# First attention: value tiles of 32 columns held stationary, its output made transposed, probabilities normalised on GpSimd

## The reference

```
def lora_linear(x, W, b, Bm, Am):
    out = jnp.einsum('bld,od->blo', x, W) + b
    upd = jnp.einsum('blr,or->blo', jnp.einsum('bld,rd->blr', x, Bm), Am)
    return out + SCALING * upd
q = _split(lora_linear(x, Wq, bq, Bq, Aq))
k = _split(lora_linear(x, Wk, bk, Bk, Ak))
v = _split(lora_linear(x, Wv, bv, Bv, Av))
scores = jnp.einsum('bhqd,bhkd->bhqk', q, k) * SCALE
attn = jax.nn.softmax(scores, axis=-1)
out = jnp.einsum('bhqk,bhkd->bhqd', attn, v)
B, H, L, hd = out.shape
out = out.transpose(0, 2, 1, 3).reshape(B, L, H * hd)
return lora_linear(out, Wo, bo, Bo, Ao)
```

## Time and profile before

| | us |
|---|---|
| median of 3 runs | 1203.41 |
| lowest to highest | 1200.97 to 1204.36 |
| the profiled execution's own time | 1205.9 |
| its span, first to last instruction | 1203.7 |
| first attention, of that span | 0 to 249.7 |

### The profile page before, as it was taken

The page is one execution under the profiler, slowest core; times in us unless marked ns, Lnnn a source line. Parts: engine busy times, 40 slices in busy tenths (PEclk is TensorE's granted clock), DMA queues, the critical chain, the costliest instruction groups (busy, mean ns, idle before and its releaser), DMA issues. The chain is left out here.

```text
span 1203.7 us, 20980 instructions
## 1 busy us (share of the span) xinstructions
PE 1084.6 (90%) x7435; PEld 977.8 (81%) x7435; DVE 683.3 (57%) x1521; ACT 469.1 (39%) x1605; POOL 201.4 (17%) x151
## 2 busy tenths in 40 slices
PE   6898988879975369999999999999999799999977
PEld 4787877769875358988889988888988689999967
DVE  6667576836868754545454545544464465545554
ACT  2554555532304314444444444444444342322322
POOL 5101010323307421111111111111111110100010
PEclk9899999888988679999999999999999899999979
DMA  6000000000005210000000000000000050000002
GB/s 257 2 2 0 0 0 1 1 19 1 0 28 168 84 37 1 2 1 1 1 0 0 0 0 0 0 0 0 1 2 1 28 211 1 0 0 0 2 1 71
DMA packets 10502, 27.73 MB, mean 23 GB/s; under 512 B 1936, under 2 KB 6960, under 8 KB 9808
## 3 DMA queue, kind: packets, MB, share of 16 engines
q1 hardware_dynamic: 9152, 26.02, 6.2%
q10 hardware_dynamic: 1296, 1.00, 0.3%
HBM read 24.91 MB, written 2.10 MB: 22 GB/s over the span
## 5 line engine op out<-in xcount | busy, mean ns | idle before, releaser
L1105 POOL TENSOR_TENSOR wa_prob<-wa_prob,wa_rsum 128x512 f32<-128x512 f32 x64 | 66.9, 1045 | 444.0 <-DVE wa_rsum L1322 444.0
L41 PE MATMUL bank<-norm_xT_hi,wide_hi 128*128 128x512 f32 x256 | 106.7, 417 | 2.2 <-ACTq L1289 2.2
L1249 ACT ACTIVATE wa_prob<-wa_prob,wa_negmax 128x128 f32<-128x128 f32 x256 | 100.0, 391 | 17.2 <-DVE wa_negmax L1311 16.8
L1348 DVE TENSOR_TENSOR le_w_or_z_lo<-bank,le_w_or_z_hi 128x512 fp32r<-128x512 f32 x64 | 44.2, 691 | 106.8 <-ACT le_w_or_z_hi L1282 106.0
L453 ACT ACTIVATE la_prob<-bank,la_negmax 128x128 f32<-128x128 f32 x256 | 90.3, 373 | 37.1 <-DVE la_negmax L508 34.3
L43 PE MATMUL bank<-norm_xT_hi,wide_lo 128*128 128x512 f32 x256 | 101.8, 398 | 0.0
L42 PE MATMUL bank<-norm_xT_lo,wide_hi 128*128 128x512 f32 x256 | 101.6, 397 | 0.0
L1264 ACT COPY wa_v<-bank 128x512 f32<-128x512 f32 x64 | 37.4, 585 | 127.7 <-PE bank L43 127.7
L132 POOL TENSOR_TENSOR norm_rstd<-norm_rstd,minus_half 128x4 f32<-128x4 f32 x23 | 23.6, 1026 | 365.3 <-DVE norm_rstd L118 365.2
L1317 DVE COPY wa_k<-bank 128x512 f32<-128x512 f32 x64 | 44.2, 691 | 68.3 <-PE bank L43 68.3
L1257 ACT COPY wa_q<-bank 128x512 f32<-128x512 f32 x64 | 37.5, 586 | 115.6 <-PE bank L43 115.6
(11 more groups left out here) (276 smaller groups left out, 2842.3 us busy)
## 6 DMA issues: line engine op xcount, KB each, us to landing
le_raw<-in_wide_w SPq DMA_DIRECT2D x16, 512.0 KB, 4.5
em_w<-in_em_w SPq DMA_DIRECT2D x1, 4096.0 KB, 15.1
x<-in_x SPq DMA_DIRECT2D x4, 512.0 KB, 4.7
lc_kt<-in_ctx_rev SPq DMA_DIRECT2D x1, 2048.0 KB, 10.8
lc_toep<-in_toeplitz SPq DMA_DIRECT2D x1, 2048.0 KB, 14.2
out_x<-x SPq DMA_DIRECT2D x8, 256.0 KB, 2.9
li_kt<-in_ctx_rev SPq DMA_DIRECT2D x1, 1536.0 KB, 7.1
la_w_raw<-in_l_w SPq DMA_DIRECT2D x1, 1024.0 KB, 6.5
```

The source lines that it names most:

```text
L41: nc.tensor.matmul(out, a[0], b[0], start=start, stop=False, skip_group_check=True)
L1105: nc.gpsimd.tensor_tensor(prob[:, s], prob[:, s], rsum[:, s, :].unsqueeze(2).to_broadcast([P, G, P]), ALU.mult).then_inc(prob_ok, 1)
L1249: last = nc.scalar.activation(prob[:, s, j, :], prob[:, s, j, :], ACT.Exp, bias=negmax[:, s, j:j + 1], scale=SCALE, accum_out=sums[:, s, j ...
L1348: nc.vector.tensor_tensor(z[1][:, t % 2, :], b_z[:, :], z[0][:, t % 2, :].bitcast(F32), ALU.subtract).then_inc(z_lo, 1)
```

## The change

- `weigh` is turned round: a head's 32 columns (its own 16 and 16 of zeros) of v are stationary, the transposed probabilities move. The result of each of the four heads goes to its own 32 partitions of the bank, already transposed, so that `turn_o` and `o` are gone and ScalarE's `keep_o` casts straight from that bank. Heads that are neighbours in a quarter differ in parity and add up. Rows of the q and k weights are reordered on the host to fit.
- The probabilities are normalised before the turn: VectorE's `inverse_sums`, then GpSimd's `normalise` over 128x512. They have three buffers instead of two.
- The row maximum is one instruction (`negate=True`); the scale has moved into `parity`, and ScalarE evacuates q.
- q and k have two buffers by group. The next group's projections are in pieces: values in units 0 and 2, q in 4 and 6, k in 8 and 10, all through one bank; the transposes of the x after that in units 13 and 14. Group 1's x is prepared ahead of the loop.
- All is written out, no loop and no register waits; units run through the groups' borders. The output bias is added in quarters.
- v has its own place beside the convolution's products, and is cleared in one piece of 4096 columns. Group 2 has the products and squares in 16 pieces on GpSimd, one a unit; the skip terms stand one a unit in group 3.
- Ahead of the first unit q comes first, then k, then v.

```diff
+    def turn_chunk(self, pe, it, c, bank):
+        for j in range(G):
+            last = self.nc.tensor.transpose(bank[:, j * P:(j + 1) * P], self.xn[:, j, c * P:(c + 1) * P],
+                                            self.pr.ident[:])
+        last.then_inc(self.s_tr, 1)
+
+    def hi_chunk(self, act, it, c, bank, out=None):
+
+        act.wait_ge(self.s_tr, DC * (self.done(it) - 1) + c + 1)
+        self.nc.scalar.copy((self.xT[0] if out is None else out)[:, c, :], bank[:, :]).then_inc(self.s_hi, 1)
...
-        q = sb("q", [P, 2, DC, GT])
-        k = sb("k", [P, DC, GT])
-
-
-        DIAG = P + HD
-        v = pr.shared[:, 0:2 * (G * H * P + P)].rearrange("p (n c) -> p n c", n=2)
-        negmax = sb("negmax", [P, 2, 4])
-        sums = sb("sums", [P, 2, H])
-        rsum = sb("rsum", [P, 2, H])
-        prob = sb("prob", [P, 2, 4, P])
+        q = sb("q", [P, 2, 2, DC, GT])
+        k = sb("k", [P, 2, DC, GT])
...
+        VW = 2 * HD
+        at = 2 * GH * NPAIR
+        v = pr.shared[:, at:at + 2 * G * H * VW].rearrange("p (i j h c) -> p i j h c", i=2, j=G, h=H)
+        NP, NS = 3, 4
+        negmax = sb("negmax", [P, NS, 4])
+        sums = sb("sums", [P, NS, 4])
+        rsum = sb("rsum", [P, NS, 4])
+        prob = sb("prob", [P, NP, 4, P])
...
+        V_AT, Q_AT, K_AT, T_AT = (0, 2), (4, 6), (8, 10), (13, 14)
+        STATS_AT, APPLY_AT, BIAS_AT = 6, 8, 9
+        HI_AT, PROJECT_AT, ADD_AT = RG + 1, RG + 2, RG + 3
...
+            def add_bias(t, j):
+                pool.wait_ge(norm.s_xn, norm.done(t))
+                own = x[:, t * G + j, :]
+                nc.gpsimd.tensor_tensor(own, own, out_bias[:], ALU.add).then_inc(xb_ok, 1)
+
+            def normalise(n):
+                pool.wait_ge(r_ok, n + 1)
+                own = prob[:, n % NP]
+                nc.gpsimd.tensor_tensor(own, own, rsum[:, n % NS, :].unsqueeze(2).to_broadcast([P, 4, P]), ALU.mult)\
+                    .then_inc(prob_ok, 1)
+
+
+            PIECES = [(d, half) for d in range(CONV_C) for half in range(2)]
+            FIRST = N - U - len(PIECES)
+
+            def conv_piece(d, half):
+                own = conv_input(pr, 0)[:, half]
+                nc.gpsimd.tensor_tensor(pr.kk[:, half, :, OFF[d]:OFF[d] + CONV_C - d], own[:, :, 0:CONV_C - d],
...
+            for n in range(N - 1):
+                g, u = divmod(n, U)
+                normalise(n + 1)
+                if g + 2 < NG and u == STATS_AT:
+                    norm.pool_rstd(pool, g + 2)
+                if g + 1 < NG and BIAS_AT <= u < BIAS_AT + G:
+                    add_bias(g + 1, u - BIAS_AT)
+                if FIRST <= n < FIRST + len(PIECES):
+                    if n == FIRST:
+                        pool.wait_ge(pr.conv_loaded, 16 * 4)
+                    conv_piece(*PIECES[n - FIRST])
+                if g == NG - 1 and u == STATS_AT:
...
+            def scores(n):
+
+                t = n // U
+                if n % U == 0:
+                    pe.wait_ge(q_ok, DC * (t + 1))
+                    pe.wait_ge(k_ok, DC * (t + 1))
+                for d in range(2):
+                    wait(pe, exp_ok, n + d - RG + 1)
...
+                    last = nc.tensor.matmul(b_v[VW * s:VW * s + VW, r // 2 * P:r // 2 * P + P],
+                                            v[:, t % 2, j, head(r, s), :], probT[:, n % 2, s, :],
+                                            start=(r == 0), stop=(r == RG - 1), skip_group_check=True)
...
+                if u in V_AT:
+                    if u == V_AT[0]:
+                        pe.wait_ge(norm.s_lo, DC * norm.split(t))
+                    else:
+                        pe.wait_ge(v_ok, 2 * t + 1)
+                    values(t, V_AT.index(u), b_p[0])
+                if u in Q_AT:
+                    if u == Q_AT[0]:
+                        pe.wait_ge(v_ok, 2 * t + 2)
+                    else:
+                        pe.wait_ge(q_ok, DC * t + 1)
+                    q_or_k(t, Q_AT.index(u), 0, b_p[0], q_ps)
+                if u in K_AT:
+                    if u == K_AT[0]:
+                        pe.wait_ge(q_ok, DC * t + 2)
+                    else:
+                        pe.wait_ge(k_ok, DC * t + 1)
+                    q_or_k(t, K_AT.index(u), 1, b_p[0], k_ps)
...
+            for n in range(N + ADD_AT):
+                g, u = divmod(n, U)
+                if n < N:
+                    turn(n)
+                    if n % 2 == 0 and n + RG < N:
+                        scores(n + RG)
+                    extra(g, u)
+                if 1 <= n <= N:
+                    weigh(n - 1)
+                b = batch_due(n, PROJECT_AT)
+                if b is not None:
+                    project(b)
...
+            def keep_q(t, m, bank):
+                act.wait_ge(q_ps, DC * t + m + 1)
+                for e in range(2):
+                    last = nc.scalar.activation(q[:, t % 2, e, m, :], bank[:, :], ACT.Identity,
+                                                bias=q_bias[:, e, m:m + 1], scale=parity[:, e:e + 1])
+                last.then_inc(q_ok, 1)
...
+            def keep_v(t, half, bank):
+
+                act.wait_ge(v_ps, 2 * t + half + 1)
+                wait(act, av_ps, U * (t - 1))
+                src = bank[:, :].rearrange("p (j h e d) -> p j h e d", j=2, e=2, d=HD)
+                own = v[:, t % 2, 2 * half:2 * half + 2].rearrange("p j (h e) c -> p j h e c", e=2)
+                for e in range(2):
+                    last = nc.scalar.copy(own[:, :, :, e, e * HD:(e + 1) * HD], src[:, :, :, e])
+                last.then_inc(v_ok, 1)
...
+            def exps(n):
+
                 act.wait_ge(max_ok, n + 1)
-                act.wait_ge(t_ps, BASE + n - 1)
-                if r == 0:
-                    act.wait_ge(av_ok, BASE + it * G + u // RG - 1)
+                wait(act, t_ps, n - NP + 1)
                 for s in range(4):
-                    h = head(r, s)
-                    last = nc.scalar.activation(prob[:, u % 2, s, :], b_s[r][:, s * P:(s + 1) * P], ACT.Exp,
-                                                bias=negmax[:, u % 2, s:s + 1], scale=SCALE,
-                                                accum_out=sums[:, j % 2, h:h + 1])
+                    last = nc.scalar.activation(prob[:, n % NP, s, :], b_s[n % RG][:, s * P:(s + 1) * P], ACT.Exp,
+                                                bias=negmax[:, n % NS, s:s + 1],
+                                                accum_out=sums[:, n % NS, s:s + 1])
...
+            for n in range(N + ADD_AT):
+                g, u = divmod(n, U)
+                b = batch_due(n, HI_AT)
+                if b is not None:
+                    keep_o(b)
+                if n + 2 < N:
+                    exps(n + 2)
+                if n < N:
+                    extra(g, u)
...
+            def row_max(n):
-                dve.wait_ge(exp_ok, RG + n - 1)
-                chain.done(nc.vector.tensor_reduce(
-                    negmax[:, u % 2, :], b_s[u % RG][:, :].rearrange("p (s k) -> p s k", s=4), AX, ALU.max))
-                nc.vector.tensor_scalar(negmax[:, u % 2, :], negmax[:, u % 2, :], -SCALE, None, ALU.mult)\
-                    .then_inc(max_ok, 1)
-
-            def keep_probT(it, u):
...
+            for n in range(N + ADD_AT + 1):
+                g, u = divmod(n, U)
+                if n + 1 < N:
+                    inverse_sums(n + 1)
+                if n + 3 < N:
+                    row_max(n + 3)
+                b = batch_due(n, HI_AT)
+                if b is not None:
+                    o_rest(b)
+                if n < N:
+                    keep_probT(n)
+                b = batch_due(n, ADD_AT)
+                if b is not None:
+                    update(b)
+                if n < N:
+                    extra(g, u)
...
-            pr.shared = sb(conv, "v_or_conv", [P, 2 * (G * 16 * P + P)])
+            pr.shared = sb(conv, "v_or_conv", [P, 6 * GH * NPAIR])
...
-    r["parity"] = np.stack([1 - odd, odd], axis=1).astype(np.float32)
+    r["parity"] = np.stack([1 - odd, odd], axis=1).astype(np.float32) * np.float32(16 ** -0.5)
```

More of the change, by code:

```diff
@@ L274, in _ @@
             xT = norm.xT
-            def q_or_k(it, n, done):
-                for m in range(DC):
-                    if n == 0:
-                        pe.wait_ge(norm.s_lo, DC * norm.split(it))
-                        pe.wait_ge(v_ok, it * 2 + m + 1)
-                    else:
-                        pe.wait_ge(q_ok, it * DC + m + 1)
-                    for c in range(DC):
-                        last = product(nc, b_p[m][:, :], pair(w, slice(None), n, c, slice(m * P, m * P + P)),
-                                       pair(xT, slice(None), c), c == 0, c == DC - 1)
-                    last.then_inc(done, 1)
@@ L288, in values @@
-            def values(it):
-                pe.wait_ge(norm.s_lo, DC * norm.split(it))
-                for half in range(2):
-                    for jj in range(2):
-                        j = 2 * half + jj
```

(34 more changed lines are left out.)

406 lines of the change are left out of this document (163 added, 243 removed).

## The result

The changed kernel takes 1163.06 us, the median of four runs (1161.64 to 1166.76), against 1203.2 us for the kernel before on the same chip (1200.97 to 1204.36): a ratio of 0.967, 95% interval 0.965 to 0.970. It is 40.1 us faster; 1156 was forecast, 1142 to 1178 was the range. The profiled execution took 1161.64 us, its span is 1159.7.

What follows compares the result with a forecast made beforehand. TensorE was taken to pace the first attention, with weighing its largest item. 31.6 + 44 + 43 + 41 + 42 = 201.6 us against 249.7, 48.1 less: 1157.8 profiled, 1156 forecast, range 1142 to 1178.

Steps and rivals of the forecast that it cites:

- Before the first turn: Start of the first attention: first turn at 36.8 - 6.6 + 1.4 = 31.6 us.
- The term of 6.6 us for the clearing: Before the first unit: VectorE's four normalisations take 1.4 instead of 8.05 us with GpSimd's clearing shortened, so 6.6 come out.
- Weighing: TensorE's products of values and probabilities: 0.5 us instead of 1.0, between ends of 0.25 and 1.0.
- The rival of better packing: Rival, chance 0.09: weighing takes 0.25 us, 12 us off where TensorE paces, result 1145 us.
- Pair length: Two units in groups 0 to 2: 4.9 us, 5.7 with an out projection; groups of 44, 43 and 41 us.
- the hole in front of the out projection shrinks: TensorE's wait at a batch's end: shorter, since only the cast and its rest stand between; no size given.
- The clock: Rival, chance 0.03: TensorE stays at its lower clock through a group, 30 us more each; 1218 us with two.
- No hole of my pairs is over 1 us: TensorE's pairs of units: no idle hole over 1 us, given as a reason against the clock staying low.
- Last group: Last batch group, paced by VectorE: 37.5 us of its work plus 4.5 for handovers and the end, 42 against 46.4.
- Contention: Rival, chance 0.07: VectorE's normalisations and skip terms each wait for a GpSimd multiplication, at most 34 us, 1190 us.
- No packing: Rival, chance 0.09: weighing stays at 1.0 us, costing 28 us over the groups, result 1186 us.
- Nothing behind the stage changes: Rest of the kernel after the first attention: its time stays the same, so only the stage's 48.1 us count.

Runs made afterwards that it cites:

- the fourfold weighing: Changed kernel with every weighing of a unit issued four times over: 1176.94 us, ratio 0.978 to the kernel before.
- the filler: Changed kernel plus eight dummy products once a group in unit 5, ahead of the weighing that waits: 1157.5 us, ratio 0.961 to the kernel before.
- odd units: Changed kernel with the next projections' pieces moved by one unit, to units 1, 3, 5, 7, 9 and 11: 1140.64 us, ratio 0.948.
- odd units with fillers: Pieces moved to odd units, plus dummy products ahead of the first two turns and in three units of the last group: 1141.35 us, ratio 0.948.
- the second bank: Changed kernel with weighed values and out projection of successive batches alternating between two banks: 1162.53 us, ratio 0.964 to the kernel before.
- the filler in unit 10: Changed kernel plus the same eight dummy products once a group, but in unit 10, where TensorE has no hole: 1169.93 us, ratio 0.972.

## Why the prediction was right, and where not

The sign, the range and the likeliest case held: the forecast of 1156 was 7 us too low. By its own steps:

- *Before the first turn*: 31.6 forecast, 30.2 measured. That miss says little: over the nine profiled kernels with this start (two have fillers ahead of the turn) it came between 30.0 and 32.0. The term of 6.6 us for the clearing is shown by itself, 7.3 us in the kernel before.
- *Weighing*: 0.5 us forecast, 0.36 measured, with 0.22 for each further four. The rival of better packing had the mechanism right (a quarter of 1.0), and the forecast sized it between its two ends, at 0.5. It did not bring 12 us: of the 10.4 us a group that the fourfold weighing adds, only 6.5 lengthen the group at the same clock, so over a third of it lies in the shadow of a wait, that for the copy in the odd units by my reading. By the same share the 0.64 us a unit that weighing lost are some 6.4 us a group, an estimate; no run brings the old weighing back alone. "TensorEngine Tiling (Array Packing)", Theoretical Speedup, of the Trainium skill gives up to four times for 32 columns. From 0.8 to 1.0 us to 0.36 is 2.2 to 2.8 times, which agrees; the further fours, at 0.22, are up to 4.5 times below the four before, so the smaller weight loads may have a part in it.
- *Pair length*: the 44, 43 and 41 us of groups 0 to 2 are what the kernel does at the full clock: 44.2, 44.5 and 43.3 with the filler. Two errors of the forecast nearly cancel there. Weighing was 0.14 too long, 2.2 us a group. And "the hole in front of the out projection shrinks" looked at the projection alone and missed that VectorE's copy and the next weighing hang on the same cast, now queued behind the copies of q (1.45 us) that the change gave to ScalarE.
- *The clock*: the step that failed. "No hole of my pairs is over 1 us" was wrong, the hole was 1.41, and with it went the full clock once in each of groups 0 to 2, some 3 us each time, 9 in all; this is what the groups took over the filler's. The rival had the mechanism and a wrong size: stretches of some 7 us, not a whole group, and no slower kernel.
- *Last group*: 42 forecast, 36.9 measured. I summed durations to 37.5 us of VectorE and it was busy 30.5. Three of the sixteen row maxima fall into the group before (13 records, 8.6 us), and the durations of instructions that follow one another overlap: the 85 records of this stretch add up to 36 us. The 4.5 us for handovers were about right (6.4 idle).
- *Contention*: 0.07 for up to 34 us. The forecast's reason against it holds: by order VectorE's normalisations and skip terms hardly meet a multiplication, and the one skip term that did took 0.52 instead of 0.34. Taking nearly all of the multiplication away changed nothing that can be told.
- *No packing*: its 1186 put all of the longer weighing on the path and left out the clock. The fourfold weighing, 1.01 a unit, measured 1177: at the same clock its groups 1 and 2 are 6.4 and 6.6 us longer where its products add 10.4, and it has no dips in them.
- *"Nothing behind the stage changes"*: the span behind it is 951.2 us (1159.7 - 208.5), before it was 954.0. From the convolution's first product to the end the twelve profiled kernels take 947.9 us (odd units) to 958.7 (odd units with fillers), though nothing there was changed, so 2.8 us are within what varies there. The clock and, in one kernel, a wait for ScalarE are part of that; the rest is open.

The sum of errors: -1.4 + 3.3 + 4.6 + 5.4 - 5.1 = 6.8 us at the stage's end, less 2.8 behind it, leaves 4 on the profiled executions (1161.64 against 1157.8).

## What to carry to other kernels

When work moves to another engine, look at what it is queued ahead of, not only at that engine's load: a 1.45 us copy ahead of a 0.37 us cast held two engines. Before a wait is removed, look for a second path to the same late instruction; here the second bank moved 11 us from one row to another and saved none. A filler or a shift by one unit is a cheap test for a clock that falls behind a hole, but judge it by the whole kernel's time, since the rest of the stage and later stages can take the gain back.

## What the runs showed of the hardware

- Four products with 32 stationary columns, each to its own quarter of the partitions, take 0.36 us and each further four 0.22, where four products with 128 stationary columns took 0.8 to 1.0. The loads of those weights are busy 2.7 us a group against 16.4.
- TensorE fell to its lower level behind a single hole of 1.41 us in a stretch in which it was busy 0.77 of 2 us; eight dummy products there kept it at 1.00 for the whole of groups 1 and 2. The size of the hole does not decide alone. With two banks it fell behind holes of 1.30 us too (81.91 and 129.44 us), while it stayed up behind one of the three holes of 1.41 with the filler in unit 10, and behind every hole of 1.06 (two each in the changed kernel, with the filler in the hole, in unit 10 and with the fourfold weighing).
- VectorE's normalisation took 1.38 us instead of 8.05 when no clearing of GpSimd's ran beside it, but 64 multiplications of 1.04 us in the same stage cost it nothing that can be measured, since they hardly meet it. One skip term that ran beside a multiplication took 0.52 us instead of 0.34. Group 1's normalisation met the biases on GpSimd and was in between:

```profile
20.51 2.98 POOL L269 TENSOR_TENSOR x<-x,la_out_bias 128x256 f32<-128x256 f32 x4
...
20.58 3.07 DVE L125 TENSOR_SCALAR norm_xn<-x,norm_meanvar,norm_rstd 128x256 f32<-128x256 f32 x4 [1.13 <-POOL norm_rstd L132]
```

  Both ended together (23.49 and 23.65). "SBUF — State Buffer", SBUF: two separate sides, of the Trainium skill speaks of an exclusive lock for a whole instruction. Strictly in turn, four bias adds (0.72 to 0.73 each by themselves, later in the stage) and four normalisations (1.38 in total) would need 4.3 us, and both were over in 3.14; GpSimd's adds were hardly slowed, 2.98 instead of 2.9. So these rows do not agree with turns of whole durations; what VectorE waited for in them is open.
